# Cross attention on one core: both halves of a batch's attention matmuls run together, behind the next batch's scores

## The chip, the core and the metric

The kernel runs on one core of a Trainium2 chip. The metric is the time on the device in microseconds (us), from a launch to the end of its last work; the profiled execution also has a span, from its first to its last instruction.

## What is computed

The program runs four transformer blocks, one after the other, on 64 sequences of 128 positions by 128 features; a context of 77 positions per sequence feeds the first three. All of them have 16 heads of 8 features. Cut to what matters here:

```python
# block 0 (cross attention + feed-forward), 1 (cross attention), 2 (cross attention + feed-forward)
scores = einsum('bhqd,bhkd->bhqk', Q, K)        # 128 x 77 per head
p = softmax(scores (causal / weighted and masked / masked))
att = einsum('bhqk,bhkd->bhqd', p, V)           # back to 128 x 128
x = layernorm(x + att (@ Wo in blocks 1 and 2)) # then the feed-forward in blocks 0 and 2
# block 3: self attention of 64-wide heads, feed-forward
```

## The kernel before, in words

The phases are A0, F0, A1, A2, F2, A3, F3: A for attention, F for a feed-forward. The change touches the cross attention phases A0, A1 and A2. Each of them walks over the 64 batches (one sequence each) as a software pipeline: every engine has a fixed list of work for one step, written by hand, and `drive` runs it for the steps -3 to 66, where `has(k)` asks whether batch b+k exists. Nothing but semaphores joins the engines, and each engine works its list strictly in the order of the code. `drive` writes the first 9 and the last steps out; the 52 steps between run in a hardware loop whose body holds four steps, so there are 13 laps of it.

The softmax of a batch is cut into two halves of eight heads, k = 0 and 1. On TensorE (PE) one step b has, in this order:

1. `scores(b+1)` (L648; ahead of it in A0 two matmuls L645 that add the causal mask): four row tiles of 32 rows. It waits for `kblk_made`, `q_kept`, `v_kept` and for the reader of the banks (`taken`), and in A2 for `keybias_made` too.
2. `attend(b-1, 1)` (L682): eight matmuls of 32 columns, four column tiles of the array, into `att_bank`. Each is two fp32 passes, which is why the trace counts 16.
3. In A1 and A2 `transpose_o(b-2)` (L701), then `transpose_p(b, 0)` (L666, eight transposes), `back(b-1)` (L693), `project_out(b-2)` (L705).
4. `project_keys(b+2)` (L620), `project_values(b+1)` (L623), `transpose_p(b, 1)` (L666), `project_queries(b+2)` (L616), `transpose_x(b+3)` (L612), and in A0 `mask_early` (L630).
5. `attend(b, 0)` (L682).

ScalarE (ACT) has in a step: `keep_att(b-1)` (L809, which waits for the second `attend` and, in A1 and A2, for L701 of the batch before), `keep_oT` (L815), the exponentials (L749), `keep_pT` for both halves (L754, it copies what L666 made and releases `attend`), `block_keys` (L769, A1 only) or `keep_k`/`keep_v`, `centre` in A1 (L800), `keep_q(b+2)` (L788, in A2 L786) and `keep_xT(b+3)` (L776). The two lines that tie `keep_q` down are

```python
            def keep_q(b, columns):
                act.wait_ge(q_made.sem(b), q_made.count(ph, b))
                if columns:
                    act.wait_ge(xT_made.sem(columns), xT_made.count(ph, columns))
```

so the copy of the queries begins only when `transpose_x`, the last write to that PSUM bank, is done too. `keep_q(b+2)` sets `q_kept`, which `scores(b+2)` waits for at the start of PE's next step. VectorE (DVE) takes the maxima and shifts (L858, L863) or, in A1, weighs (L871), masks and takes the maxima; GpSimd (POOL) shifts in A1 and does the norms; SyncE issues the DMAs.

Of the kernel before, what the change touches and what calls it, by code (L numbers as in the profile page):

```python
# [138 lines left out]
def build_layers(nc, a, out):  # L139
# [3 lines left out]
    with ExitStack() as ctx:  # L143
# [453 lines left out]
        def cross_tensor(pe, ph):  # L597
# [4 lines left out]
            def out_banks_left(b):  # L602

                if prev in FFS:
                    last = Batch(GROUPS // 2 - 1, 1)
                    pe.wait_ge(ft_made.sem(last), ft_made.count(prev, last))
                elif prev:
                    wait_earlier(pe, sum_made, ph, b, 1)

            def transpose_x(b):  # L610
                pe.wait_ge(X_loaded.sem(b), X_loaded.count(ph, b))
                nc.tensor.transpose(out_bank[:, X_COL:X_COL + T], x_s[b.par][:], ident[:]).then_inc(xT_made.sem(b), 1)  # L612

            def project_queries(b):
                pe.wait_ge(xT_kept.sem(b), xT_kept.count(ph, b))
                nc.tensor.matmul(out_bank[:, Q_COL:Q_COL + T], w["wq"][:], xT_s[b.par][:], start=True, stop=True).then_inc(q_made.sem(b), 1)  # L616

            def project_keys(b):
                pe.wait_ge(ctx_loaded.sem(b), ctx_loaded.count(ph, b))
                nc.tensor.matmul(k_col_bank[:, K_COL:K_COL + C], w["wk"][:], ctx_s[b.par][:], start=True, stop=True).then_inc(k_made.sem(b), 1)  # L620

            def project_values(b):
                nc.tensor.matmul(v_bank[0:C, V_COL:V_COL + D], ctx_s[b.par][:], w["wv"][:], start=True, stop=True).then_inc(v_made.sem(b), 1)  # L623

            def mask_early(b, values):
                pe.wait_ge(k_kept.sem(b), k_kept.count(ph, b))
                if values:
                    pe.wait_ge(v_kept.sem(values), v_kept.count(ph, values))
                for c in range(2):
                    nc.tensor.matmul(bank[c][:, 0:QC], identb[:], causal[:], start=True, stop=False)  # L630

            def scores(b):
                pe.wait_ge(kblk_made.sem(b), kblk_made.count(ph, b))
                pe.wait_ge(q_kept.sem(b), q_kept.count(ph, b))

                if (b + -1).exists:
                    pe.wait_ge(v_kept.sem(b + -1), v_kept.count(ph, b + -1))
                if ph == "A2":
                    pe.wait_ge(keybias_made.sem(b), keybias_made.count(ph, b))

                if (b + -1).exists:
                    pe.wait_ge(taken.sem(b + -1), taken.count(ph, b + -1, 1))
                if ph == "A0":
                    for c in range(2, NQ):
                        nc.tensor.matmul(bank[c][:, 0:QC], identb[:], causal[:], start=True, stop=False)  # L645
                for c in range(NQ):
                    rows = slice(32 * c, 32 * c + 32)
                    mm = nc.tensor.matmul(bank[c][:, 0:QC], qT_s[b.par][rows, :], kblk_s[b.par][rows, :],  # L648
                                          start=(ph != "A0"), stop=(ph != "A2"))
                if ph == "A2":  # L650
                    for c in range(NQ):
                        row = slice(32 * c, 32 * c + 1)
                        bias = keybias_s[b.par][row, :].unsqueeze(1).to_broadcast([1, QH, C])
                        mm = nc.tensor.matmul(bank[c][:, 0:QC], onesb[row, :], bias, start=False, stop=True)
                mm.then_inc(s_made.sem(b), 1)

            def transpose_p(b, k):
                pe.wait_ge(exp_made.sem(b), exp_made.count(ph, b, k))

                if k == 1:  # L660
                    pe.wait_ge(pT_kept.sem(b), pT_kept.count(ph, b, 0))
                elif (b + -1).exists:
                    pe.wait_ge(pT_kept.sem(b + -1), pT_kept.count(ph, b + -1, 1))
                for h in range(2 * QH):
                    head = k * 2 * QH + h
                    mm = nc.tensor.transpose(two[0:C, h * T:(h + 1) * T], p_s[b.par][:, head * C:(head + 1) * C], ident[:])  # L666
                mm.then_inc(pT_made.sem(b), 1)

            def attend(b, k):
                pe.wait_ge(pT_kept.sem(b), pT_kept.count(ph, b, k))  # L670
                if k == 0:
                    pe.wait_ge(v_kept.sem(b), v_kept.count(ph, b))

                    if (b + -1).exists:
                        pe.wait_ge(att_kept.sem(b + -1), att_kept.count(ph, b + -1))
                    if ph != "A0" and (b + -2).exists:
                        pe.wait_ge(sum_made.sem(b + -2), sum_made.count(ph, b + -2))
                for j in range(2):
                    for i in range(4):
                        first = (4 * k + i) * VPAIR + 32 * j  # L680
                        h = 2 * i + j
                        mm = nc.tensor.matmul(att_bank[32 * i:32 * i + 32, k * T:(k + 1) * T], v_s[b.par][:, first:first + 32],  # L682
                                              pT_s[k][:, h * T:(h + 1) * T], start=(j == 0), stop=(j == 1))
                mm.then_inc(att_made.sem(b), 1)

            def back(b, columns):
                pe.wait_ge(att_kept.sem(b), att_kept.count(ph, b))

                if columns:
                    pe.wait_ge(xT_kept.sem(columns), xT_kept.count(ph, columns))  # L690
                for c in range(2):
                    col = BACK_COL + c * T
                    mm = nc.tensor.transpose(out_bank[:, col:col + T], att_s[b.par][:, c * T:(c + 1) * T], ident[:])  # L693
                mm.then_inc(back_made.sem(b), 1)

            def transpose_o(b, attending):
                pe.wait_ge(o_made.sem(b), o_made.count(ph, b))

                if not attending:
                    pe.wait_ge(sum_made.sem(b + -1), sum_made.count(ph, b + -1))  # L700
                nc.tensor.transpose(att_bank[:, OT_COL:OT_COL + T], o_s[b.par][:], ident[:]).then_inc(oT_made.sem(b), 1)  # L701

            def project_out(b):
                pe.wait_ge(oT_kept.sem(b), oT_kept.count(ph, b))
                nc.tensor.matmul(att_bank[:, O_COL:O_COL + D], oT_s[b.par][:], w["wo"][:], start=True, stop=True).then_inc(proj_made.sem(b), 1)  # L705

            def step(b, has):
                if has(1):
                    scores(b + 1)
                if has(-1):  # L710
                    attend(b + -1, 1)
                if has(-2) and ph != "A0":
                    transpose_o(b + -2, has(1))
                if has(0):
                    transpose_p(b, 0)
                if has(-1):
                    back(b + -1, b + 2 if has(2) else None)
                if has(-2) and ph != "A0":
                    project_out(b + -2)

                if has(1):
                    pe.wait_ge(taken.sem(b + 1), taken.count(ph, b + 1, 0))
                if has(2):
                    project_keys(b + 2)
                if has(1):
                    project_values(b + 1)
                if has(0):
                    transpose_p(b, 1)

                if has(-1):  # L730
                    pe.wait_ge(o_made.sem(b + -1), o_made.count(ph, b + -1))
                elif has(3) and not has(2):
                    out_banks_left(b + 3)
                if has(2):
                    project_queries(b + 2)
                if has(3):
                    transpose_x(b + 3)
                if has(2) and ph == "A0":
                    mask_early(b + 2, b + 1 if has(1) else None)
                if has(0):  # L740
                    attend(b, 0)
            drive(pe, NB, step, reach=REACH)

        def cross_scalar(act, ph):
# [1291 lines left out]
```

## Time and profile before

| what | us |
| --- | --- |
| median of 3 runs | 2608.63 (2605.84 to 2609.42) |
| profiled execution, its own time | 2601.15 |
| its span | 2599.3 |
| mean granted TensorE clock, share of full | 0.982 |
| PE busy, whole span | 2368.9 (91%) |
| `scores` from the first to the last batch, A0 | 14.8 to 412.4 |
| the same, A1 | 559.6 to 985.1 |
| the same, A2 | 1023.3 to 1398.6 |

The three ranges are the starts of L648 for the first and the last batch of the phase. A step of A0 takes some 6.2 us, one of A1 some 6.8 us, one of A2 some 5.9 us. A row of the trace has its start, its length, the engine, the line and what is written from what; the starts of two rows give the time between them whatever the lengths, which for matmuls are modelled and overlap.

### The profile page before, as it was taken

The page shows a single profiled execution, that of the slowest core. Times are in us where ns is not written, and L with a number is a line of the kernel's source. Part 1 is how long each engine was busy: PE and PEld are TensorE (multiplying, and loading weights), DVE is VectorE, ACT ScalarE, POOL GpSimd, SP SyncE. Part 2 cuts the span into 40 slices and gives each one's busy share as a digit, 9 for nine tenths or more (in the row PEclk, how much of TensorE's full clock was granted, in tenths as well). Part 3 has the DMA queues.
Part 4 walks back from the last instruction along what each step waited for, and adds up shares of the span by engine and source line. Part 5 has one row for each costly group of instructions (what it writes and reads, how often), then busy time and mean ns, then how long its engine had stood idle before and what let it go on. Part 6 is the DMA issues. An engine that isn't in the chain of part 4 may idle for free. (4 is left out here: it accounts for less than half of the span.)

```text
span 2599.3 us, 82853 instructions
## 1 busy us (share of the span) xinstructions
PE 2368.9 (91%) x26670; PEld 1807.7 (70%) x26670; DVE 1894.2 (73%) x4003; ACT 1502.3 (58%) x3407; POOL 1537.1 (59%) x2438
## 2 busy tenths in 40 slices
PE   6999998987777777999998988999999999999899
PEld 4666666966565665777776876777777777777587
DVE  4676763139999995777775667888888888888566
ACT  4777776558888884777776533444444444444343
POOL 2555555127888884555556776666666666666332
PEclk8999999989999997999999999999999999999999
DMA  4111111234445441221111213333333333333121
GB/s 121 37 38 38 38 39 46 70 115 149 153 147 156 150 150 47 44 47 47 46 46 41 67 57 95 93 96 96 92 92 92 93 92 92 92 93 92 46 58 55
DMA packets 443043, 211.78 MB, mean 81 GB/s; under 512 B 206400, under 2 KB 433856, under 8 KB 442816
## 3 DMA queue, kind: packets, MB, share of 16 engines
q1 hardware_dynamic: 442944, 210.51, 30.3%
q8 instruction: 56, 0.92, 0.1%
q14 instruction: 43, 0.35, 0.0%
HBM read 113.36 MB, written 29.88 MB: 55 GB/s over the span
## 5 line engine op out<-in xcount | busy, mean ns | idle before, releaser
L666 PE MATMUL bank<-sb_ident,sb_region 128*77 128x128 f32 x3072 | 414.3, 278 | 85.5 <-ACT sb_pT L754 84.5
L666 PEld LDWEIGHTS bank<-sb_ident,sb_region 128*77 128x77 f32 x3072 | 350.8, 151 | 139.8 <-issue 137.6
L754 ACT ACTIVATE sb_pT<-bank 77x1024 f32<-77x1024 f32 x384 | 391.0, 1018 | 67.6 <-PE bank L666 67.6
L858 DVE TENSOR_REDUCE sb_max<-bank 128x8 f32<-128x616 f32 x256 | 203.5, 795 | 206.8 <-PE bank L648 118.2
L1517 ACT ACTIVATE sb_l<-sb_l 128x640 f32<-128x640 f32 x128 | 94.4, 737 | 402.2 <-DVE sb_l L1565 402.2
L749 ACT ACTIVATE sb_region<-sb_region 128x616 f32<-128x616 f32 x384 | 276.7, 720 | 1.4 <-POOL sb_region L995 1.4
L1638 POOL TENSOR_TENSOR sb_pn<-sb_l,sb_r_all 128x512 f32<-128x512 f32 x128 | 134.5, 1051 | 231.8 <-DVE sb_r_all L1575 228.0
L1398 PE MATMUL bank<-sb_region,sb_wqkv 128*128 128x128 f32 x2048 | 253.4, 277 | 1.1 <-ACT sb_region L1526 0.7
L682 PE MATMUL bank<-sb_pT,sb_v 77*32 77x128 f32 x6144 | 248.6, 280 | 3.5 <-ACT sb_pT L754 3.2
L1432 PE MATMUL bank<-sb_wvo,sb_region 128*64 128x512 f32 x1024 | 247.9, 605 | 0.0
L1398 PEld LDWEIGHTS bank<-sb_region,sb_wqkv 128*128 128x128 f32 x2048 | 241.9, 194 | 3.6 <-ACT sb_region L1526 1.3
L682 PEld LDWEIGHTS bank<-sb_pT,sb_v 77*32 77x32 f32 x6144 | 145.0, 109 | 119.9 <-issue 69.9
L1629 POOL TENSOR_TENSOR sb_region<-sb_region 128x512 f32<-128x512 f32 x128 | 162.7, 1271 | 93.3 <-PE bank L1418 79.9
L863 DVE TENSOR_TENSOR sb_region<-bank,sb_max 128x616 f32<-128x616 f32 x256 | 204.7, 800 | 11.6
L648 PE MATMUL bank<-sb_region,sb_qT 32*128 32x308 f32 x1536 | 158.0, 481 | 59.9 <-issue 41.5
L995 POOL TENSOR_TENSOR sb_region<-sb_region,sb_max 128x616 f32<-128x616 f32 x128 | 156.3, 1221 | 67.9 <-DVE sb_max L884 67.9
L1005 POOL TENSOR_TENSOR sb_var<-sb_mv,sb_ln_eps 128x1 f32<-128x1 f32 x192 | 36.8, 192 | 267.0 <-DVE sb_mv L935 267.0
L1501 ACT ACTIVATE sb_region<-bank 128x512 f32<-128x512 f32 x256 | 152.4, 597 | 43.4 <-PE bank L1432 42.2
L1553 DVE TENSOR_TENSOR sb_region<-bank,sb_cosT 128x512 f32<-128x512 f32 x256 | 173.0, 676 | 3.5 <-PE bank L1398 3.3
L1460 PEld LDWEIGHTS bank<-sb_region,sb_pT 128*64 128x64 f32 x2048 | 120.3, 137 | 78.7 <-issue 70.3
L1184 ACT ACTIVATE sb_fh<-bank,sb_L_xattn_ffb 128x256 f32<-128x256 f32 x256 | 109.3, 472 | 113.0 <-PE bank L1135 113.0
L1553 DVE TENSOR_TENSOR sb_region<-bank,sb_sinT 128x512 f32<-128x512 f32 x256 | 174.3, 681 | 0.0
(183 smaller groups left out, 5652.1 us busy)
## 6 DMA issues: line engine op xcount, KB each, us to landing
sb_region<-in_side SPq DMA_DIRECT2D x64, 616.0 KB, 3.8
sb_pT<-sb_region SPq DMA_DIRECT2D x512, 64.0 KB, 2.1
sb_kF<-sb_region SPq DMA_DIRECT2D x512, 64.0 KB, 2.1
scratch_after_A<-sb_y SPq DMA_DIRECT2D x256, 64.0 KB, 1.7
sb_fx<-scratch_after_A SPq DMA_DIRECT2D x96, 128.0 KB, 2.1
sb_mask<-in_mask SPq DMA_DIRECT2D x64, 154.0 KB, 2.2
sb_x<-scratch_after_F SPq DMA_DIRECT2D x128, 64.0 KB, 1.8
sb_ctx<-in_ctxT SPq DMA_DIRECT2D x192, 38.5 KB, 1.9
```

The costliest lines, as they stand in the source:

```text
L648: mm = nc.tensor.matmul(bank[c][:, 0:QC], qT_s[b.par][rows, :], kblk_s[b.par][rows, :], start=(ph != "A0"), stop=(ph != "A2"))
L666: mm = nc.tensor.transpose(two[0:C, h * T:(h + 1) * T], p_s[b.par][:, head * C:(head + 1) * C], ident[:])
L682: mm = nc.tensor.matmul(att_bank[32 * i:32 * i + 32, k * T:(k + 1) * T], v_s[b.par][:, first:first + 32], pT_s[k][:, h * T:(h + 1) * T], s ...
L749: nc.scalar.activation(half(p_s[b.par], k), half(p_s[b.par], k), ACT.Exp, scale=SCALE[ph]).then_inc(exp_made.sem(b), 1)
L754: nc.scalar.activation(pT_s[k][:], two[0:C, :], ACT.Copy).then_inc(pT_kept.sem(b), 1)
L858: nc.vector.tensor_reduce(dst, by_bank_and_head(scores_half(k)), AX.X, ALU.max).then_inc(max_made.sem(b), 1)
L863: nc.vector.tensor_tensor(by_bank_and_head(by_bank(half(p_s[b.par], k))), by_bank_and_head(scores_half(k)), spread_max(k), ALU.subtract).t ...
L995: nc.gpsimd.tensor_tensor(by_head(half(p_s[b.par], k)), by_head(half(p_s[b.par], k)), spread(max_s[:, 8 * k:8 * k + 8], C), ALU.subtract)\
L1398: mm = nc.tensor.matmul(rope_bank[eo][:, n * T:(n + 1) * T], wqkv[:, col:col + 128], xnT_s[b.lap], start=True, stop=True)
L1432: mm = nc.tensor.matmul(vo_banks[g][r * SEG:(r + 1) * SEG, :], xnT_s[b.lap][:, g * SEG:(g + 1) * SEG], wvo[:, (2 * h + r) * HC * D:(2 * h ...
L1553: ins = nc.vector.tensor_tensor(part[what][eo].rearrange("p (n t) -> p n t", t=T), src, table[:].unsqueeze(1).to_broadcast([128, BLOCKS, T ...
L1629: nc.gpsimd.tensor_tensor(turned[what][0][:], ropeC[what][0][:], ropeS[what][1][:], ALU.subtract).then_inc(added.sem(b), 1)
```

## The change

In the step of PE `attend(b, 0)` goes from the end of step b, behind `project_queries`, `transpose_x` and `mask_early`, to step b+1, behind `scores(b+2)` and right ahead of `attend(b, 1)`. Nothing is added or taken away, and no other engine's list changes.

```diff
@@ -708,6 +708,7 @@
                 if has(1):
                     scores(b + 1)
                 if has(-1):
+                    attend(b + -1, 0)
                     attend(b + -1, 1)
                 if has(-2) and ph != "A0":
                     transpose_o(b + -2, has(1))
@@ -737,8 +738,6 @@
                     transpose_x(b + 3)
                 if has(2) and ph == "A0":
                     mask_early(b + 2, b + 1 if has(1) else None)
-                if has(0):
-                    attend(b, 0)
             drive(pe, NB, step, reach=REACH)
```

The list of PE in A0, from the end of one step into the next, as a difference (`v_kept`, `q_kept` and so on are the semaphores waited for; `shifted` is `taken` in A0):

```order
 L630 MATMUL bank<-sb_causal,sb_identb 128x308 [waits v_kept,k_kept]
 L630 MATMUL bank<-sb_causal,sb_identb 128x308
-L682 MATMUL bank<-sb_pT,sb_v 32x128 [waits att_kept,v_kept,pT_kept]
-L682 MATMUL bank<-sb_pT,sb_v 32x128 x7
 L645 MATMUL bank<-sb_causal,sb_identb 128x308 [waits v_kept,shifted,q_kept,kblk_made]
 L645 MATMUL bank<-sb_causal,sb_identb 128x308
 L648 MATMUL bank<-sb_region,sb_qT 128x308 x4
+L682 MATMUL bank<-sb_pT,sb_v 32x128 [waits att_kept,v_kept,pT_kept]
+L682 MATMUL bank<-sb_pT,sb_v 32x128 x7
 L682 MATMUL bank<-sb_pT,sb_v 32x128 [waits pT_kept]
 L682 MATMUL bank<-sb_pT,sb_v 32x128 x7
```

The eight matmuls of the first half no longer stand between the early mask (L630) and the first instruction that waits for `q_kept`; they stand behind the scores, with nothing between them and the second half.

The list of PE in the loop of A1, from the projection of the queries (L616) into the next step, before:

```order
L616 MATMUL bank<-sb_xT,sb_L_xattn_wq 128x128 [waits xT_kept,o_made]
L612 MATMUL bank<-sb_ident,sb_x 128x128 [waits X_loaded_1]
L682 MATMUL bank<-sb_pT,sb_v 32x128 [waits att_kept,sum_made,v_kept,pT_kept]
L682 MATMUL bank<-sb_pT,sb_v 32x128 x7
L642 REGISTER_ALU [waits v_kept,q_kept,kblk_made]
L648 MATMUL bank<-sb_region,sb_qT 128x308 [waits s_weighted]
L648 MATMUL bank<-sb_region,sb_qT 128x308 x3
L682 MATMUL bank<-sb_pT,sb_v 32x128 [waits pT_kept]
```

and the same place in the changed kernel:

```order
L616 MATMUL bank<-sb_xT,sb_L_xattn_wq 128x128 [waits xT_kept,o_made]
L612 MATMUL bank<-sb_ident,sb_x 128x128 [waits X_loaded_1]
L642 REGISTER_ALU [waits v_kept,q_kept,kblk_made]
L648 MATMUL bank<-sb_region,sb_qT 128x308 [waits s_weighted]
L648 MATMUL bank<-sb_region,sb_qT 128x308 x3
L682 MATMUL bank<-sb_pT,sb_v 32x128 [waits att_kept,sum_made,v_kept,pT_kept]
L682 MATMUL bank<-sb_pT,sb_v 32x128 x7
L682 MATMUL bank<-sb_pT,sb_v 32x128 [waits pT_kept]
L682 MATMUL bank<-sb_pT,sb_v 32x128 x7
L701 MATMUL bank<-sb_ident,sb_o 128x128 [waits o_made]
```

Here the transpose of the output (L701), for which ScalarE's L809 waits, moves behind both halves instead of one.

## Rows read from the trace of the kernel before

**Rows 1.** Loops of A0, A1, A2: us; PE, PEld, DVE, ACT, POOL busy; TensorE clock; DMA

```profile
33.00:406.00 373.00, 346.57 (x4080) 241.79 (x4073) 254.02 (x589) 261.35 (x532) 208.60 (x407) 0.99 0.18 50
592.00:985.00 393.00, 308.89 (x3943) 236.41 (x3943) 358.28 (x698) 324.35 (x757) 321.33 (x466) 1.00 0.50 150
1043.00:1398.00 355.00, 327.37 (x4303) 251.31 (x4302) 254.59 (x597) 264.04 (x598) 207.84 (x413) 1.00 0.20 46
```

**Rows 2.** Waits of ScalarE and VectorE, 592:985 (A1): total us, times, longest

```profile
ACT sb_region L809 <- PE bank L701: 62.3, 52, 1.3
DVE sb_region L871 <- PE bank L648: 28.0, 57, 1.0
```

**Rows 3.** Timeline of a step in A0

```profile
306.17 0.37 ACT L788 ACTIVATE sb_qT<-bank,sb_L_xattn_bq 128x128 f32<-128x128 f32 x1 [0.63 <-PE bank L612]
306.30 0.64 PE L682 MATMUL bank<-sb_pT,sb_v 77*32 77x128 f32 x16
306.88 0.43 PE L645 MATMUL bank<-sb_causal,sb_identb 128*128 128x308 bf16 x2
...
307.24 0.80 PE L648 MATMUL bank<-sb_region,sb_qT 32*128 32x308 f32 x8
...
307.97 0.65 PE L682 MATMUL bank<-sb_pT,sb_v 77*32 77x128 f32 x16
...
308.55 1.10 PE L666 MATMUL bank<-sb_ident,sb_region 128*77 128x128 f32 x8
```

**Rows 4.** Timeline of A0, the step at whose end the loop closes

```profile
312.33 0.37 ACT L788 ACTIVATE sb_qT<-bank,sb_L_xattn_bq 128x128 f32<-128x128 f32 x1 [0.65 <-PE bank L612]
...
313.23 0.43 PE L645 MATMUL bank<-sb_causal,sb_identb 128*128 128x308 bf16 x2
```

**Rows 5.** Timeline of a step in A1

```profile
801.36 0.64 PE L682 MATMUL bank<-sb_pT,sb_v 77*32 77x128 f32 x16
...
802.26 0.38 ACT L788 ACTIVATE sb_qT<-bank,sb_L_xattn_bq 128x128 f32<-128x128 f32 x1
...
802.83 0.80 PE L648 MATMUL bank<-sb_region,sb_qT 32*128 32x308 f32 x8 [0.83 <-issue]
...
803.56 0.64 PE L682 MATMUL bank<-sb_pT,sb_v 77*32 77x128 f32 x16
...
804.13 0.33 PE L701 MATMUL bank<-sb_ident,sb_o 128*128 128x128 f32 x1
...
804.58 0.38 ACT L809 ACTIVATE sb_region<-bank 128x256 f32<-128x256 f32 x1 [1.17 <-PE bank L701]
...
809.01 0.38 ACT L788 ACTIVATE sb_qT<-bank,sb_L_xattn_bq 128x128 f32<-128x128 f32 x1
...
809.62 0.80 PE L648 MATMUL bank<-sb_region,sb_qT 32*128 32x308 f32 x8 [0.86 <-issue]
```

**Rows 6.** Timeline of a step in A2

```profile
1249.95 0.65 PE L682 MATMUL bank<-sb_pT,sb_v 77*32 77x128 f32 x16
...
1250.08 0.28 ACT L786 ACTIVATE sb_qT<-bank 128x128 f32<-128x128 f32 x1 [0.72 <-PE bank L612]
...
1250.64 0.80 PE L648 MATMUL bank<-sb_region,sb_qT 32*128 32x308 f32 x8
```

**Rows 7.** Timeline of A2, the step at whose end the loop closes

```profile
1279.72 0.28 ACT L786 ACTIVATE sb_qT<-bank 128x128 f32<-128x128 f32 x1 [0.74 <-PE bank L612]
...
1280.45 0.80 PE L648 MATMUL bank<-sb_region,sb_qT 32*128 32x308 f32 x8 [0.24 <-issue]
```

**Rows 8.** Timeline of A2: two passes, then another operation, both full tiles

```profile
1253.11 0.38 PE L693 MATMUL bank<-sb_ident,sb_region 128*128 128x128 f32 x2
...
1253.33 0.39 PE L705 MATMUL bank<-sb_L_xattn_wo,sb_oT 128*128 128x128 f32 x2
```

**Rows 9.** All matmuls of line 682: min/median/max ns of one, first and last start

```profile
L682 PE MATMUL bank<-sb_pT,sb_v x6144: 272/273/423, 26.4 to 1410.2; 77*32 77x128 f32 x199
```

## The prediction

> **What bounds the kernel now.** I read the busy times of the three loops first, then the waits of each engine in them, then single steps in the timeline, since the change moves work inside a step and its worth is decided by what waits in that step. In the loops of A0 and A2 TensorE is busy 347 of 373 us and 327 of 355 us, in A1 only 309 of 393 us, where VectorE has 358 and ScalarE 324 [rows 1]. So in A0 and A2 PE's own list nearly sets the step. In A1 no engine is full, and the step is a loop through several of them: ScalarE waits 62.3 us in 52 steps, 1.2 us each, for PE's L701, and VectorE 0.5 us each time for the scores [rows 2]. One step of A1 shows the loop [rows 5]: PE starts the scores at 802.83, the second half of attend at 803.56, L701 at 804.13; ScalarE, idle for 1.17 us, begins its list with L809 at 804.58 and comes to the copy of the queries (L788) at 809.01; that ends at 809.39, and the scores of the next batch start at 809.62. PE was idle for 0.86 us ahead of them. Everything from 802.83 to 809.62 hangs together, and the first half of attend (801.36, over by about 801.94) stands in PE's idle time, in no part of this loop.
>
> **What is removed.** The first half of attend leaves its place ahead of the scores. One attend occupies PE for 0.58 us from start to start (306.30 to 306.88, 307.97 to 308.55) [rows 3]. What PE can do with the gap is limited by `q_kept`: the copy of the queries is released by PE's `transpose_x`, the instruction just ahead of the place (ScalarE idle until L612 [rows 3]), and ends only after it.
>
> The time from the end of that copy to the scores, where PE was idle and waiting, is 802.64 to 802.83 and 809.39 to 809.62, so 0.19 and 0.23 us [rows 5]. I take 0.20. For A2, which has one semaphore more to wait for, I take 0.25; its own row allows 0.28 (1250.36 to 1250.64 [rows 6]), though there the end of attend may have set the start. Bounds: 0.18 and 0.28.
>
> - A0, usual step: the copy ends at 306.17 + 0.37 = 306.54, so L645 can start at 306.74 in place of 306.88: 0.14 us sooner [rows 3]. Where the hardware loop closes, PE starts late after attend for the branch: the copy ends at 312.70, L645 starts at 313.23 [rows 4]. With the branch under the wait instead, it starts at 312.90: 0.33 sooner.
> - A2, usual step: 1250.36 + 0.25 = 1250.61 for 1250.64, 0.03 sooner [rows 6]. At the closing of the loop 1280.00 + 0.25 = 1280.25 for 1280.45, 0.20 sooner [rows 7].
> - A1: the scores already wait for the copy with PE idle; nothing is won.
>
> A step counts if it has scores and an attend of an earlier batch: steps 1 to 62, 62 in each phase, of which 12 close the loop (13 laps). Won: A0 50 x 0.14 + 12 x 0.33 = 11.0 us; A2 50 x 0.03 + 12 x 0.20 = 3.9 us; together 14.9 us.
>
> **What is added.** The same half now stands behind the scores, ahead of the second half. PE goes from the scores to attend, and from attend to L666 or L701, with no idle time named in any of the rows [rows 3, 5], so whatever the half costs there pushes the transposes. In A0 and A2 the copy L754 and the second L666 follow from them, in A1 the whole list of ScalarE from L809 on, and with it the next copy of the queries. VectorE and POOL are driven by the scores and have slack: VectorE waits for them in A1 even now [rows 2].
>
> How much the half costs there no row shows, because two attends never follow each other. From above: 0.58 us, as alone. But 0.58 holds a share that belongs to the change of shape. One fp32 pass of 128 columns takes 0.11 us where full tiles follow full tiles (L693, two passes, to L705: 0.22 [rows 8]); four column tiles with four passes each are 4 x 0.107 = 0.43 us if the tiles run beside each other. The rest, 0.15 us, falls only where the shape changes, and between two attends it doesn't. From below: the 16 rows of one attend lie in 0.64 us, and a single one is 0.273 long [rows 3, 9], so the starts spread over 0.37 us. I take 0.43, since the neighbours of equal shape in [rows 8] show no gap, and keep 0.37 and 0.58 as the ends.
>
> The Trainium skill, "TensorEngine Tiling (Array Packing)", Key Properties, says that a change of tiling mode, not of the tile alone, drains the array; no run here shows two attends in a row yet, and by that rule one drain in each step would be saved. "TensorE: Matmul & The Clock Gate", Part 1, puts the least distance between two starts at about 25 ns; an estimate from it is 16 x 25 ns = 0.40 us, and the sum would be 186 x 0.40 - 14.9 = 59.5 us. The rows agree with that distance (0.37 us over 15 gaps [rows 3, 9]).
>
> **The sum.** 3 x 62 = 186 steps x 0.43 = 80.0 us added, less 14.9 us won: +65.1 us. By phase: A0 +15.7, A1 +26.7, A2 +22.8. The profiled execution's own 2601.15 us becomes 2666. It lies 7.5 us below the median of the runs, so for the median I add the sum to 2608.63: 2673.7, say 2674 us. The feed-forward phases and A3 keep their times; they only start later. One early wait of A0 for a context load would swallow 1 to 2 us, which I leave in the range. The bounds together: least 186 x 0.37 with the shortest wait (0.18 us in A0 and A2: won 8.0 + 4.2 + 5.0 + 3.2 = 20.4) gives +48; most 186 x 0.58 with the longest (0.28: won 3.0 + 3.0 + 0 + 2.0 = 8.0) gives +100.
>
> **The rivals.**
> - *The half costs its full 0.58 us in the new place* (a gap between the two halves, from their separate waits or because the 0.15 us belongs to attend itself). 186 x 0.58 - 14.9 = +93 us: 2702. For it: all attends in the trace are 0.58 us from what follows; against it: equal shapes in [rows 8] follow without a gap. Chance 0.27.
> - *The half is hidden in the new place*, since the transposes behind it would have waited anyway; then only the earlier scores are left and the kernel is faster by 14.9 us: 2594. It would need 0.43 us of idle time on PE between the scores and the transposes. Rows 3 and 5 have none, and ScalarE stands waiting for L701. Chance 0.03.
> - *The second half pays itself back: PE isn't held by `q_kept`.* The step would become shorter by 0.58 and longer by 0.43, 186 x 0.15 = 28 us faster: 2581. It decides from a wait under 0.15 us; the rows of A0 give 306.74 - 306.30 = 0.44 us. Chance 0.01.
> - *The clock falls* as PE idles more in each step. A1 has PE idle for a fifth of the time at a granted clock of 1.00, the full 2.4 GHz [rows 1], and after the change A0 and A2 are still busier than that. Chance 0.02, above 2720.
> - *The bound lies partly elsewhere and takes up more than half of it* (+5 to +45 us): VectorE at 91% of A1 would have to be the one that sets it, yet it waits for the scores. Chance 0.04.
>
> **The numbers.** The forecast has 0.63 (its own range +54 to +76 us: 2663 to 2685). With the first rival, 0.90 lie between +48 and +100; the range is 2656 to 2706. A measurement can tell 0.2%, 5 us, from no change. Faster 0.04, the same 0.01, slower 0.95.
>
> **What the profile would show.** A usual step would be longer by 0.29 us in A0, 0.43 in A1 and 0.40 in A2, in A1 from the 6.79 of [rows 5] to 7.22. PE would be idle for some 0.4 us ahead of L645 in A0 and 0.6 us ahead of L648 in A2, until the copy of the queries is done, and ScalarE's wait ahead of L809 in A1 would grow from 1.2 to 1.6 us. The 32 matmuls of both halves would lie in about 1.07 us (0.64 + 0.43), in the first rival 1.22. I am wrong in the mechanism if the scores of A0 start right behind L630 without idle time, or if A1's step keeps its length; wrong in size if the two attends are 0.58 us apart.

## The result: slower by 4.9%, twice the forecast

The changed kernel takes 2733.85 us (median, 2733.0 to 2734.78), the kernel before in the same comparison 2607.24 us: a ratio of 1.0486 (95% interval 1.0469 to 1.0502), +127 us. The forecast was +65 us with a range that ended at 2706 us; the direction was right, the time lies outside the range.

The page of the changed kernel:

```profile
span 2732.6 us, 82866 instructions
...
PE 2406.0 (88%) x26670; PEld 1881.4 (69%) x26670; DVE 1897.3 (69%) x4003; ACT 1509.7 (55%) x3407; POOL 1527.2 (56%) x2438
...
PEclk9999999988888888799999998999999999999999
```

PE's busy time rose by 37 us though it does the same 26670 matmuls. In the eight of the forty slices that lie over A1 the granted clock stands at 8, in the one behind them, the passage to A2, at 7; before the change, where a slice is 65 us and not 68, only the one in which A1 begins (8) and that of the passage (7) stood below 9:

```profile
PEclk8999999989999997999999999999999999999999
```

(Below line 711 the numbers of the changed kernel's lines are up to one lower: L808 is the L809 of before, L787 is L788, L785 is L786.)

Where the time went, by the start of the scores of the first batch of each phase, which ended the stretch before it:

| stretch | before, us | after, us | longer | forecast |
| --- | --- | --- | --- | --- |
| A0 and F0 | 14.8 to 559.6 | 14.9 to 574.3 | 14.6 | 15.7 |
| A1, and what leads to A2 | 559.6 to 1023.3 | 574.3 to 1129.0 | 91.0 | 26.7 |
| A2, to the last scores | 1023.3 to 1398.6 | 1129.0 to 1530.0 | 25.7 | 22.8 |

Together 131 of the 133.3 us between the two profiled executions. Two phases are within 3 us of their terms. The miss is in A1, 64 us.

Busy times and granted clock of the three loops after the change, in the columns of [rows 1], and under them two neighbouring steps of A1, from scores to scores, and two short stretches of the second of these:

```profile
33.00:419.00 386.00, 324.96 (x4070) 242.51 (x4069) 253.66 (x589) 261.04 (x530) 207.33 (x407) 1.00 0.18 48
608.00:1078.00 470.00, 365.16 (x3907) 293.56 (x3911) 357.59 (x693) 327.58 (x751) 306.44 (x462) 0.84 0.43 126
1150.00:1529.00 379.00, 317.54 (x4286) 254.17 (x4275) 254.37 (x597) 263.00 (x596) 210.97 (x413) 1.00 0.19 43
...
799.43:806.63 7.20, 5.20 (x69) 4.14 (x69) 6.22 (x14) 5.59 (x14) 5.44 (x8) 1.00 0.49 144
806.63:816.21 9.58, 8.21 (x69) 6.67 (x69) 5.96 (x13) 5.81 (x14) 4.91 (x8) 0.64 0.35 105
...
807.00:810.00 3.00, 3.00 (x41) 1.69 (x38) 2.01 (x3) 0.21 (x1) 2.36 (x5) 0.50 0.23 71
814.00:816.00 2.00, 0.84 (x8) 0.60 (x6) 1.88 (x4) 2.00 (x6) 1.57 (x3) 1.00 0.12 20
```

A1 had a clock of 1.00 before [rows 1], now 0.84; A0 and A2 keep 1.00. The first of the two steps, at the full clock, is 7.20 us long; the forecast had 7.22. The second takes 9.58 us for the same instructions, at a mean granted clock of 0.64: from 807 to 810 us the clock stands at 0.50, the level of 1.2 GHz, and from 814 to 816 us at 1.00, that of 2.4 GHz. Between the scores at 604.18 and those at 1085.68, 23 steps are of the second kind (9.45 to 9.82 us), the others 7.07 to 7.31 us. 23 x 2.45 us is 56 us; one more slow step (588.16 to 597.33, 9.17 us, where a step took 6.1 us before) comes at the start of the phase, +3 us. The remaining 5 us lie behind A1: from its last scores to the first of A2 it takes 43.4 us (1085.68 to 1129.04) where it took 38.2 (985.10 to 1023.26).

PE's timeline in these two steps:

```profile
799.43 0.80 PE L648 MATMUL bank<-sb_region,sb_qT 32*128 32x308 f32 x8 [1.55 <-issue]
800.16 1.08 PE L682 MATMUL bank<-sb_pT,sb_v 77*32 77x128 f32 x32
801.17 0.33 PE L701 MATMUL bank<-sb_ident,sb_o 128*128 128x128 f32 x1
801.34 1.04 PE L666 MATMUL bank<-sb_ident,sb_region 128*77 128x128 f32 x8
...
803.82 1.07 PE L666 MATMUL bank<-sb_ident,sb_region 128*77 128x128 f32 x8 [0.60 <-ACT sb_pT L753]
804.73 0.39 PE L616 MATMUL bank<-sb_xT,sb_L_xattn_wq 128*128 128x128 f32 x2
804.95 0.27 PE L612 MATMUL bank<-sb_ident,sb_x 128*128 128x128 f32 x1
806.63 1.31 PE L648 MATMUL bank<-sb_region,sb_qT 32*128 32x308 f32 x8 [1.40 <-issue]
807.87 1.94 PE L682 MATMUL bank<-sb_pT,sb_v 77*32 77x128 f32 x32
809.73 0.48 PE L701 MATMUL bank<-sb_ident,sb_o 128*128 128x128 f32 x1
810.00 1.91 PE L666 MATMUL bank<-sb_ident,sb_region 128*77 128x128 f32 x8
```

The 32 matmuls of both halves are 1.08 us long and L701 starts 1.01 us after their first, as 0.58 + 0.43. Ahead of the scores PE is idle for 1.40 us; before the change it was 0.83 to 0.86 [rows 5]. The scores that begin at 806.63 end at half speed, and what follows is slow: L682 takes 1.94 in place of 1.08 us, L666 1.91 in place of 1.04. The scores and L682 lie on the path to L701, for which ScalarE waits first, and L666 on that to the copy of the transposes, for which it waits next. The waits of ScalarE for L701 in A1 show it, 2.3 us each time in the mean against 1.2 in [rows 2]:

```profile
ACT sb_region L808 <- PE bank L701: 118.9, 52, 3.4
```

### The profile page after: what moved, and what is told of

Same layout as the page of the kernel before. It is cut to its first block, busy times and chain, and to the rows that moved or that the text cites. A ratio compares the mean times of both kernels' runs of the same rounds, so it can differ in the third digit from the quotient of the medians.

```text
span 2732.6 us, 82866 instructions
## 1 busy us (share of the span) xinstructions
PE 2406.0 (88%) x26670; PEld 1881.4 (69%) x26670; DVE 1897.3 (69%) x4003; ACT 1509.7 (55%) x3407; POOL 1527.2 (56%) x2438
## 4 chain that ended last, share of the span: by engine, by line
PE 66%; issue 11%; ACT 7%; SPq 6%; DVE 4%; POOL 3%; DMA 1%; ACTq 0%; DVEq 0%; POOLq 0%
PE bank L666 11%; PE bank L682 8%; PE bank L1431 7%; PE bank L1397 7%; PE bank L648 6%; PE bank L1134 5%; ACT sb_pT L753 4%; PE bank L1148 4%; PE bank L1459 3%; PE bank L1417 3%; PE bank L1441 2%; SPq L1339 2%; SPq L1342 2%; DVE sb_max L857 1%; PE bank L701 1%
## 5 line engine op out<-in xcount | busy, mean ns | idle before, releaser
L666 PE MATMUL bank<-sb_ident,sb_region 128*77 128x128 f32 x3072 | 435.7, 288 | 86.7 <-ACT sb_pT L753 85.8
L666 PEld LDWEIGHTS bank<-sb_ident,sb_region 128*77 128x77 f32 x3072 | 375.0, 159 | 135.8 <-issue 133.8
L648 PE MATMUL bank<-sb_region,sb_qT 32*128 32x308 f32 x1536 | 170.2, 515 | 131.8 <-issue 68.3
L682 PEld LDWEIGHTS bank<-sb_pT,sb_v 77*32 77x32 f32 x6144 | 169.4, 117 | 93.6 <-issue 48.6
L682 PE MATMUL bank<-sb_pT,sb_v 77*32 77x128 f32 x6144 | 229.3, 294 | 3.2 <-ACT sb_pT L753 3.2
L808 ACT ACTIVATE sb_region<-bank 128x256 f32<-128x256 f32 x192 | 73.8, 384 | 249.9 <-PE bank L701 172.2
L648 PEld LDWEIGHTS bank<-sb_region,sb_qT 32*128 32x128 f32 x1536 | 65.8, 196 | 178.4 <-issue 126.8
```

## The experiments

The theory from this profile was: the terms of the forecast hold, and on top of them TensorE's clock falls in A1 because PE idles more there. Its rival: the order itself costs A1 more, through ScalarE's waits, and the clock only goes along. All ratios are to the kernel before, with 95% intervals.

**The change in A0 and A2 alone.**

```diff
                 if has(-1):
+                    if ph != "A1":
+                        attend(b + -1, 0)
                     attend(b + -1, 1)
...
-                if has(0):
+                if has(0) and not (ph != "A1"):
                     attend(b, 0)
```

> The change in A0 and A2 alone; A1 has the order of before. Theory clock (the forecast's terms are right, and what it missed is TensorE's clock, which falls in A1 alone because PE idles there in one piece ahead of the scores): A1 is as before, with a granted clock of 1.00 and steps of 6.79 us, and what is left is the 14.6 and 26.1 us that A0 and A2 are longer in the changed kernel's trace, some +41 us, ratio 1.016. Rival (A0 and A2 leave something behind that A1 pays for, a later load or a cooler clock): A1 still loses a part of its 91 us, ratio 1.025 or more.

2646.83 us, 1.0164 (1.0147 to 1.0181), +41.3 us. In A1 ScalarE's wait for L701 is what it was before the change, and the clock of the stretch is 1.00:

```profile
ACT sb_region L811 <- PE bank L701: 62.3, 52, 1.3
...
620.00:960.00 340.00, 267.07 (x3408) 204.03 (x3408) 309.24 (x602) 279.82 (x652) 277.14 (x402) 1.00 0.51 151
```

A0 and A2 leave nothing behind that the steps of A1 pay for. The passage from A1's last scores to A2's first takes 43.1 us here too, so its 5 us don't come from the new order in A1; what sets its length is not shown.

**The change in A1 alone.**

```diff
                 if has(-1):
+                    if ph == "A1":
+                        attend(b + -1, 0)
                     attend(b + -1, 1)
...
-                if has(0):
+                if has(0) and not (ph == "A1"):
                     attend(b, 0)
```

> The change in A1 alone; A0 and A2 have the order of before. Theory clock: A1 is longer by 91 us as in the changed kernel, with steps of 7.20 us at the full clock and of about 9.7 us where it falls; ratio 1.035. Rival (the phases hang together): clearly less than 1.035.

2686.61 us, 1.0318 (1.0297 to 1.0340), +81 us, a little under the 91 us of the stretch in the changed kernel. The clock falls here as well:

```profile
620.00:960.00 340.00, 265.19 (x2799) 213.49 (x2798) 256.84 (x497) 235.10 (x541) 221.65 (x331) 0.83 0.42 125
```

From 600 us on, 22 steps of A1 are longer than 8 us (one of 8.11, the others 9.42 to 9.88 us), 23 in the changed kernel, and there is no slow step ahead of them. So the number of falls differs a little from kernel to kernel, and with it the cost of A1. The two parts together give 41 + 81 = 122 us of 127: the phases cost what they cost alone.

**The first half done twice in A1**, once without a signal at its old place and once behind the scores. The step has one attend more, and nothing less.

```diff
+                if has(0) and ph == "A1":
+                    attend(b, 0, again=True)   # no then_inc
```

> The changed kernel, but in A1 PE also does the matmuls of the first half at their old place, without a signal, so that work is added and none taken away: A1 has three attends in a step. It fills 0.6 us of the 1.4 us in which PE idles ahead of the scores. Theory clock: the granted clock of A1 goes back to about 1.00, all its steps are 7.2 us, A1 is longer than before by 27 us instead of 91, and the total is +68 us, ratio 1.026, although PE does more. Rival (the 91 us come from the order, through ScalarE waiting for PE, and the clock only goes along with it): no better than the changed kernel, ratio 1.049 or more.

2674.20 us, 1.0263 (1.0246 to 1.0280): 60 us faster than the changed kernel, with more work. The clock of A1 is 1.00:

```profile
620.00:960.00 340.00, 271.32 (x3953) 212.19 (x3951) 295.88 (x566) 263.30 (x612) 256.82 (x377) 1.00 0.48 142
```

Against the kernel with the change in A0 and A2 alone it is 27.4 us slower; the forecast's term for A1 is 26.7. The rival is out: with the same order the path costs 27 us, and the rest comes and goes with the clock.

**One matmul more in A1**, 0.21 us, at the old place of the first half; its result is never read.

```diff
+            def fill(b, n):                      # waits for att_kept(b-1) and sum_made(b-2)
+                for _ in range(n):
+                    nc.tensor.matmul(att_bank[:, 0:T], ident[:], ident[:], start=True, stop=True)
...
+                if has(0) and ph == "A1":
+                    fill(b, 1)
```

> The changed kernel with a single fp32 matmul of 128 columns (0.21 us, two passes, its result never read) in A1 at the old place of the first half, behind the transpose of x. Theory clock: it shortens the idle time, so it gives back a part of the 64 us or all of it; ratio between 1.026 and 1.049, and the fewer steps run at a fallen clock the nearer to 1.026. Rival (the order): ratio 1.049 as for the changed kernel.

2671.43 us, 1.0259 (1.0242 to 1.0276). Less work than the run before added (0.21 us for an attend of 0.58) gives back as much, and PE still idles for 1.2 to 1.4 us ahead of the scores, where it was 1.4 to 1.6 in the changed kernel:

```profile
620.00:960.00 340.00, 255.41 (x3286) 208.61 (x3284) 295.78 (x564) 262.88 (x611) 256.21 (x377) 0.99 0.48 141
```

**The same kind of work in the kernel before**, two such matmuls in A1 ahead of the first half: `fill(b, 2)`.

> The kernel before, with two fp32 matmuls of 128 columns (0.43 us, never read) in A1 between the transpose of x and the first half of attend, where PE idles ahead of the scores. A control for the two runs with added work. Theory clock: nothing is won here, since A1's clock is at 1.00 already, and nothing is lost, since the work lies in PE's idle time; ratio 1.000. Rival (added work ahead of the scores speeds A1 up by itself, or costs): ratio off 1.000 by more than 0.002.

2606.12 us, 1.0011 (1.0002 to 1.0021). Added work there brings nothing where the clock is full: the interval has it 0.5 to 5.5 us slower.

**One matmul between the two halves**, in all three phases, on top of the run with the first half done twice.

```diff
                     attend(b + -1, 0)
+                    nc.tensor.matmul(att_bank[:, T:2 * T], identb[:], identb[:], start=True, stop=True)
                     attend(b + -1, 1)
```

> The changed kernel with the first half done again at its old place in A1 (as in the run before of that name, ratio 1.0263), and in A0, A1 and A2 one bf16 matmul of 128 columns over the full array between the two halves (0.05 us of columns, overwritten by the second half). Theory shape change (0.15 us of the 0.58 us of an attend fall where the tile shape changes, so two attends in a row spare it): the matmul brings two changes of shape back, 0.10 into the column tiles and 0.15 out, with its own 0.05 us 0.30 us in each of 186 steps, +56 us, ratio 1.048. Rival (the second attend is cheaper for another reason, such as weights loaded ahead): only 0.05 to 0.1 us each, +10 to +19 us, ratio 1.030 to 1.034.

2728.37 us, 1.0471 (1.0455 to 1.0487), 54 us slower than the run without it, 0.29 us for each of 186 steps. PE's timeline in A1:

```profile
801.57 0.65 PE L682 MATMUL bank<-sb_pT,sb_v 77*32 77x128 f32 x16
802.14 0.23 PE L713 MATMUL bank<-sb_identb 128*128 128x128 bf16 x1
802.30 0.64 PE L682 MATMUL bank<-sb_pT,sb_v 77*32 77x128 f32 x16
802.88 0.33 PE L702 MATMUL bank<-sb_ident,sb_o 128*128 128x128 f32 x1
```

0.57, 0.16 and 0.58 us from start to start: 1.31 for what takes 1.01 without the small matmul, 0.30 more. That is the forecast's reading of an attend, 0.43 us of work and 0.15 for the change of shape, and the rule of the Trainium skill, "TensorEngine Tiling (Array Packing)", Key Properties: the array drains when the tiling mode changes. The trace agrees, with 0.25 us for the two changes beside 0.05 us of columns (an estimate: in A0 two bf16 matmuls of 308 columns, L630, take 0.42 us and one 0.29, so 128 columns take 0.13 x 128 / 308).

**The second half and L701 ahead of the scores**, in A1 of the kernel before.

```diff
-                if has(1):
+                if has(1) and ph != "A1":
                     scores(b + 1)
                 if has(-1):
                     attend(b + -1, 1)
                 if has(-2) and ph != "A0":
                     transpose_o(b + -2, has(1))
+                if has(1) and ph == "A1":
+                    scores(b + 1)
```

> The opposite change, in A1 alone, to the kernel before: the second half of attend and the transpose of the output go ahead of the next batch's scores, so that both halves are done before them. If the loop PE to ScalarE sets A1's step (scores, second half, L701, then ScalarE's list up to the copy of the queries), taking the scores and the second half out of it must shorten the step, until VectorE's list (6.3 us) sets it: about 6.4 us in place of 6.79, 62 steps, -20 to -25 us, ratio 0.991. Rival (the loop is only seemingly closed, and VectorE sets A1 now): the scores come 0.4 us later behind ScalarE's copy of the second half, and A1 gets longer by up to 62 x 0.4 us, ratio up to 1.010.

2610.09 us, 1.0020 (1.0011 to 1.0029). I expected 1% faster. The steps of A1 now alternate between 6.42 or 6.49 us and 7.25 or 7.37 us (792.82 to 800.07 and 800.07 to 806.56 are two of them); four in a row take 6.88 us in the mean, against 6.79 in [rows 5]. New waits have taken the place of the old one:

```profile
ACT sb_region L751 <- POOL sb_region L997: 58.2, 53, 1.6
...
PE bank L682 <- ACT sb_pT L756: 11.7, 27, 0.4
PE bank L616 <- DVE sb_o L917: 9.7, 26, 0.5
```

ScalarE waits for POOL's second shift instead of for PE, and in every second step PE's projection of the queries waits for VectorE, which got its scores later. The short steps have the length that was expected of the shorter loop, which is no proof of it, since short and long ones come in turn; which of the two waits makes the long ones is not settled.

**L701 alone ahead of the scores**, in A1 of the kernel before.

```diff
+                if has(-2) and ph == "A1":
+                    transpose_o(b + -2, has(1))
                 if has(1):
                     scores(b + 1)
                 if has(-1):
                     attend(b + -1, 1)
-                if has(-2) and ph != "A0":
+                if has(-2) and ph == "A2":
                     transpose_o(b + -2, has(1))
```

> The kernel before, with the transpose of the output (L701) of A1 moved ahead of the next batch's scores, into the 0.8 us in which PE idles there. ScalarE's list then starts behind the second half of attend alone, some 0.3 us sooner (804.25 in place of 804.58 in the rows of the step before). If the loop PE to ScalarE sets A1's step, 62 steps get 0.2 to 0.3 us shorter, -12 to -18 us, ratio 0.993 to 0.995. Rival (VectorE's list sets it, or ScalarE's list then waits for POOL's second shift as in the run with the second half early): no gain, ratio 0.999 to 1.002.

2597.99 us, 0.9973 (0.9963 to 0.9984): faster than both kernels, by about half of what was expected. The timeline of a step:

```profile
698.93 0.33 PE L701 MATMUL bank<-sb_ident,sb_o 128*128 128x128 f32 x1
...
699.84 0.80 PE L648 MATMUL bank<-sb_region,sb_qT 32*128 32x308 f32 x8 [0.58 <-issue]
...
700.57 0.65 PE L682 MATMUL bank<-sb_pT,sb_v 77*32 77x128 f32 x16
...
701.43 0.39 ACT L811 ACTIVATE sb_region<-bank 128x256 f32<-128x256 f32 x1 [1.02 <-PE bank L682]
```

L701 now lies in PE's idle time, and ScalarE's list starts 1.59 us after the scores, where it was 1.75 us (802.83 to 804.58 [rows 5]): 0.16 us a step. The 0.3 us that I expected left out that ScalarE starts only 0.21 us after the row of the last attend ends (701.22 to 701.43). The loop from PE to ScalarE is the bound of A1, as the forecast had it.

**One matmul more in A1 at another place**, behind the projection of the values, so that the idle time ahead of the scores is hardly touched; and then **two** of them there.

```diff
                 if has(1):
                     project_values(b + 1)
+                if has(1) and ph == "A1":
+                    pe.wait_ge(taken.sem(b + 1), taken.count(ph, b + 1, 1))
+                    nc.tensor.matmul(bank[3][:, 384:512], ident[:], ident[:], start=True, stop=True)
```

> The changed kernel with the same single fp32 matmul of 128 columns (0.21 us) per step of A1 as in the run with one matmul, but behind the projection of the values, where PE idles 0.6 us ahead of the second transposes. The idle time ahead of the scores stays at 1.4 us. Theory amount of work (what brings the clock back is PE's work in a step, wherever it lies): A1 at a granted clock of about 1.00, ratio 1.026. Theory long gap (what fells the clock is the 1.4 us in one piece ahead of the scores): the clock still falls, ratio 1.04 to 1.049.

2692.61 us, 1.0343 (1.0323 to 1.0364) with one. The same stretch of A1:

```profile
620.00:960.00 340.00, 268.39 (x3146) 220.71 (x3142) 278.98 (x537) 251.99 (x582) 243.29 (x359) 0.91 0.46 135
```

> As the run with one matmul behind the projection of the values of A1, but two of them (0.43 us of 0.6 us of idle time), so that nothing ahead of the scores changes. The single one brought the granted clock of A1's loop from 0.83 to 0.91 only, where the same matmul ahead of the scores brought it to 0.99. Theory amount of work: twice the work brings the clock to 1.00 here too, ratio 1.024 to 1.027. Theory long gap (the 1.4 us in one piece ahead of the scores must be cut): the clock stays near 0.91 and the ratio near 1.034.

2676.26 us, 1.0270 (1.0253 to 1.0287) with two:

```profile
620.00:960.00 340.00, 272.09 (x3373) 226.64 (x3373) 290.55 (x560) 261.83 (x606) 253.74 (x374) 0.97 0.47 140
```

With two, PE is still idle for 1.2 to 1.6 us ahead of the scores, and the clock is nearly back. So the long gap as such doesn't fell the clock; the amount of work in a step counts. But the place counts as well: 0.21 us bring 0.99 ahead of the scores and 0.91 here, though the gap ahead of the scores hardly differs (1.2 and 1.3 us in most steps). Why is open.

## Why the prediction was wrong, by its own steps

- *A1 is a loop from PE through ScalarE, and attend's first half stood outside it.* Right. ScalarE's wait ahead of L809 grew, and the step at the full clock is 7.20 us (forecast 7.22).
- *The cost of the half in its new place, 0.43 us.* Right: 1.01 us for both, and the run with a matmul between them shows the change of shape as the 0.15 us that is spared. The rival with 0.58 us is out.
- *What the earlier scores win.* Right for A0's usual step, 6.42 to 6.50 us for 6.14 to 6.22 (forecast +0.29). Too much where the hardware loop closes. The forecast had the branch hidden under the wait and the scores 0.20 us (in A2 0.25) behind the end of the copy; it is 0.33 us in A0 (322.35 to 322.68 in the rows below) and 0.43 us in A2 (1326.34 to 1326.77). So a closing step of A0 is 0.24 us longer and not 0.10, one of A2 0.41 and not 0.23. That A0 and F0 together still come to 14.6 us for 15.7 is in part luck: A0's first seven steps, up to the scores at 65.00 before and at 63.51 after, got 1.6 us shorter, where the sum had them some 1.5 us longer. In A2, 25.7 us for 22.8, the usual step wins nothing either: the time from the end of the copy to the scores is 0.28 us there and not 0.25 (L785 ends at 1332.87, L648 starts at 1333.15; L900, which the profile names, had ended at 1332.80). The two terms are 50 x 0.03 = 1.5 and 12 x 0.18 = 2.2 us. The rows of the changed kernel:

```profile
321.98 0.37 ACT L787 ACTIVATE sb_qT<-bank,sb_L_xattn_bq 128x128 f32<-128x128 f32 x1 [0.64 <-PE bank L612]
...
322.68 0.43 PE L645 MATMUL bank<-sb_causal,sb_identb 128*128 128x308 bf16 x2 [0.52 <-ACT sb_qT L787]
...
1332.59 0.28 ACT L785 ACTIVATE sb_qT<-bank 128x128 f32<-128x128 f32 x1 [0.72 <-PE bank L612]
1332.61 0.19 DVE L900 TENSOR_SCALAR sb_keybias<-sb_keymask 128x77 bf16<-128x77 int32 x1
...
1333.15 0.80 PE L648 MATMUL bank<-sb_region,sb_qT 32*128 32x308 f32 x8 [0.62 <-DVE sb_keybias L900]
```

- *"The clock falls as PE idles more in each step": chance 0.02.* This is the step that failed: a term of some 59 us, the slow steps of A1, was put at nothing in the sum. It argued that A1 had a fifth of PE's time idle at a clock of 1.00, and that A0 and A2 stay busier than that after the change. Both are true, and say nothing of A1 itself, which was the least busy phase and became less busy: 0.79 of the time before [rows 1], 5.20 of 7.20 us or 0.72 in a step at the full clock now. The forecast added 0.43 us to A1's step and did not ask what PE's share would be then. Shown by the runs: with the order of the change and a little more work on PE the same stretch of A1 has a clock of 0.99 to 1.00 and costs 27 us; without it 0.83, and 81 to 91 us. The rival's line, above 2720 us, is where the time came out (2733.85), but no row stood behind that figure. What PE's work in a step has to be for the full clock, and why its place matters, stays open.

The Trainium skill, "TensorE: Matmul & The Clock Gate", Part 1, says that the clock has two levels and that how busy PE has been lately chooses between them. The trace agrees with the two levels: 0.50 and 1.00 within one step. The runs agree that PE's work matters, 0.99 and 1.00 with added work for 0.83 without; that one matmul brings less at another place they show beside it.

The range ended at 2706 us, 97 above the median before, where the bounds of the sum gave 100; that decides nothing.

## What to carry to other kernels

Work that an engine does while it waits for another is free only there: before moving it, ask what stands idle at the old place and what is late at the new one; here 0.6 us left an idle stretch and 0.43 us entered the loop that sets the step. In a phase where TensorE isn't full, work out its busy share after the change as well as the step: a longer step with the same work can cost its clock, and then costs about three times its own length (27 us of path, 81 and 91 us measured). Instructions that keep the tile shape of the one before are cheaper than alone, here 0.43 for 0.58 us.

## What the runs showed that I had not expected

- A phase of TensorE at 0.79 busy ran at the full clock; the same work in steps 6% longer fell to half of it for a part of 23 steps, and a single matmul of 0.21 us per step, a result that nobody reads, made the kernel 62 us faster (2733.85 to 2671.43).
- The same 0.21 us brought the mean clock of the stretch to 0.99 at one place and to 0.91 at another, 2 us earlier in the step (646.37 and 644.30, in steps that begin at 640.74 and 640.68).
- A fall costs far more than what seems to start it: the 0.5 us by which PE's idle time ahead of the scores grew (0.86 to 1.40 us) stands beside 2.4 us for each slow step, in which ScalarE and VectorE wait as well.
